# One core, a routed low-rank layer folded into one wide matmul: h transposed by transfers inside SBUF and by VectorE, three tiles behind, with the loads of x on ScalarE's queue

## The chip, the cores and the metric

The kernel runs on one core of a Trainium2 chip. Its time is the device time in microseconds (us); three runs gave 165.15, 165.2 and 165.34, so the median is 165.2 us.

## The reference

x has 128 batch rows, 32 tokens of each, 512 features. Each token goes through a linear layer with a routed low-rank part and then through a matrix of signs, and is added to x:

```
base   = x W^T
logits = x Wr^T + 5 * one_hot(itok)              # 8 experts
gates  = softmax over the top 2 logits, 0 elsewhere
h      = x A^T                                   # 8 experts x 16 ranks = 128 columns
c      = base + 2 * sum_e gates_e * (h_e B_e^T)
out    = x + (c sign) * softplus(scale)
```

All tensors are fp32.

## The kernel before

**What is folded.** Since nothing nonlinear stands between W and sign, the kernel makes M = W^T sign * softplus(scale) + I once, and B2 = B sign * 2 softplus(scale) once. A tile is one token of all 128 batch rows. For each tile it computes x times a matrix of 648 columns, which are Wr (8), A (128) and M (512): that is `wide`. It then makes the gated h (128 columns) and adds h_gated B2 to the M part: that is `lora`. Each fp32 factor is split into a high and a low part, and three products stand for one (high x high, high x low, low x high). So `wide` is 4 chunks of features x 3 products x 2 PSUM banks (392 and 256 columns) = 24 matmuls, and `lora` is 3 x 2 = 6.

**What each engine does for a tile t.** The queues run in program order and meet by semaphores.
- SyncE loads x(t) in four transfers of 64 KB (L227) and stores y (L233).
- VectorE transposes x in 32x32 blocks (L432, `turn_x`). The layout of the load makes the block transpose a full one.
- ScalarE makes the high part of x (L348, `high_x`), GpSimd the low part (L300, `low_x`).
- TensorE runs `wide` (L643) into the two banks `pair[t % 3]`. When the bank with Wr and A is done it signals `head_ready`.
- VectorE then makes logits (L516), the top two (L524, L532), the gates (L537 to L547, with ScalarE's exponential L385 between) and h_gated (L551).
- TensorE transposes h_gated against `ident` into the PSUM tile `p_ht` (L686, `turn_h`). ScalarE makes its high part ht_hi (L381), VectorE its low part ht_lo (L507, `low_h`).
- TensorE runs `lora` (L679) into the same banks, and ScalarE copies them to y (L394, L395).

**How the steps are staggered.** Step s of TensorE does the first half of wide(s), then lora(s-2), then the second half of wide(s), and last the transpose of h_gated(s-1), at the end of the step. LAG = 2 is that distance, S3 = 3 the number of buffers of everything, LEAD = 2 says that x is prepared two tiles ahead. Step s of VectorE begins with the logits of tile s-1 when TensorE starts step s. The middle steps run in a hardware loop. `finish` is a written-out end for tiles 30 and 31, in which the banks with the head come first.

**The front.** TensorE warms up on zeros (L577, into `p_b2`), makes M (L589 to L571) and B2 (L626, L630), and then `first_tile` (L668). VectorE, ScalarE and GpSimd split W, sign, B and M. softplus(scale) is a chain of eight small VectorE instructions (L448 to L457) with two exponentials on ScalarE.

## Time and profile before

| | |
|---|---|
| median of three runs | 165.2 us |
| the profiled execution, its own time | 164.64 us |
| span of that execution | 162.8 us |
| PE busy | 158.3 us (97%), 1070 matmuls |
| VectorE busy | 97.6 us (60%) |
| ScalarE busy | 66.0 us (41%) |
| GpSimd busy | 52.1 us (32%) |
| chain that ended last | PE 90% |

The page gives busy time by engine, the chain of work that ended last, groups of instructions with what ended the idle time before them, and the transfers. Matmuls are pipelined: one is shown as longer than the distance to the next. What a matmul costs is therefore read from the distance between starts, or from the pieces of the chain, and not from its duration.

### The profile page before, as it was taken

To read this page: it belongs to the slowest core of one execution; us is meant where nothing else is said; L and a number is where in the kernel's file an instruction comes from. 1 tells how busy PE (TensorE), PEld (TensorE's weight loads), DVE (VectorE), ACT (ScalarE), POOL (GpSimd) and SP (SyncE) were. 2 spreads that over 40 slices of the span, in tenths; PEclk is the share of its full clock that TensorE was granted. 3 is DMA by queue.
4 is the path that set the end of the run, shared out by engine and by line. 5 is a ranking of instruction groups with operands and counts; after the bars stand their busy time and mean duration, and the time that the engine had idled before them with its cause. 6 is when DMAs were issued, how large, how long until landed. Compare 5 with 4: busy or idle time off the path is not lost.

```text
span 162.8 us, 3711 instructions
## 1 busy us (share of the span) xinstructions
PE 158.3 (97%) x1070; PEld 153.8 (94%) x1070; DVE 97.6 (60%) x416; ACT 66.0 (41%) x177; POOL 52.1 (32%) x50
## 2 busy tenths in 40 slices
PE   7999998999999999999999999999999999999993
PEld 5788897999999999999999999999999999999992
DVE  5689997555556665554554555556665555455741
ACT  3654722434344333344444343344333344443440
POOL 2994453332222233333333322222333333333000
PEclk9999999999999999999999999999999999999998
DMA  4996323424333333334333333333333333111113
GB/s 170 380 146 136 90 82 101 131 70 146 105 122 114 124 119 115 124 129 129 129 129 127 104 101 117 112 121 123 113 123 120 128 129 129 64 64 64 68 66 129
DMA packets 29431, 19.51 MB, mean 120 GB/s; under 512 B 7248, under 2 KB 24432, under 8 KB 29424
## 3 DMA queue, kind: packets, MB, share of 16 engines
q1 hardware_dynamic: 28496, 18.23, 36.5%
q10 hardware_dynamic: 928, 1.20, 2.0%
q8 instruction: 3, 0.05, 0.1%
q14 instruction: 4, 0.03, 0.1%
HBM read 11.03 MB, written 8.39 MB: 119 GB/s over the span
## 4 chain that ended last, share of the span: by engine, by line
PE 90%; DVE 7%; issue 1%; ACT 0%; DVEq 0%
PE pair L643 66%; PE pair L679 14%; PE p_b L577 2%; PE p_ht L686 2%; PE pair L589 2%; DVE m_full L470 2%; PE pair L596 2%; PE pair L603 2%; DVE xt L432 1%; DVE wide_lo L476 1%; DVE gate L547 1%; DVE b_lo L501 0%; DVE b_lo L487 0%; DVE wide_lo L483 0%; ACT y L395 0%
## 5 line engine op out<-in xcount | busy, mean ns | idle before, releaser
L300 POOL TENSOR_TENSOR xt_lo<-xt,xt_hi 128x512 fp32r<-128x512 f32 x32 | 41.6, 1299 | 91.5 <-ACT xt_hi L348 91.5
L643 PE MATMUL pair<-wide_hi,xt_hi 128*128 128x392 f32 (+1 forms) x248 | 60.8, 321 | 0.0
L643 PE MATMUL pair<-wide_hi,xt_lo 128*128 128x392 f32 (+1 forms) x248 | 58.3, 311 | 0.0
L643 PE MATMUL pair<-wide_lo,xt_hi 128*128 128x392 f32 (+1 forms) x248 | 58.3, 311 | 0.0
L643 PEld LDWEIGHTS pair<-wide_hi,xt_lo 128*128 128x128 f32 x248 | 38.6, 188 | 0.0
L643 PEld LDWEIGHTS pair<-wide_lo,xt_hi 128*128 128x128 f32 x248 | 38.5, 188 | 0.0
L643 PEld LDWEIGHTS pair<-wide_hi,xt_hi 128*128 128x128 f32 x248 | 38.3, 189 | 0.1
L394 ACT ACTIVATE y<-pair 128x256 f32<-128x256 f32 x31 | 11.9, 384 | 44.3 <-PE pair L679 44.3
L516 DVE TENSOR_TENSOR logits<-pair,bias 128x8 f32<-128x8 f32 x32 | 5.3, 165 | 35.7 <-PE pair L643 35.7
L432 DVE STREAM_TRANSPOSE xt<-x_in 128x512 f32<-128x512 f32 x32 | 22.7, 710 | 3.7 <-DVE top L524 3.2
L348 ACT ACTIVATE xt_hi<-xt 128x512 fp32r<-128x512 f32 x32 | 20.3, 633 | 2.8 <-DVE xt L432 2.8
L381 ACT ACTIVATE ht_hi<-p_ht 128x128 fp32r<-128x128 f32 x32 | 8.9, 277 | 22.6 <-PE p_ht L686 22.6
L507 DVE TENSOR_TENSOR ht_lo<-p_ht,ht_hi 128x128 fp32r<-128x128 f32 x32 | 9.3, 290 | 13.6 <-ACT ht_hi L381 13.6
L385 ACT ACTIVATE e<-top 128x1 f32<-128x1 f32 x32 | 9.5, 296 | 14.4 <-DVE top L524 14.3
L551 DVE SCALAR_TENSOR_TENSOR h_gated<-pair,rdenom,gate 128x128 f32<-128x128 f32 x32 | 11.2, 350 | 3.3
L679 PE MATMUL pair<-b_hi,ht_hi 128*128 128x256 f32 x64 | 13.0, 281 | 0.0
L679 PE MATMUL pair<-b_lo,ht_hi 128*128 128x256 f32 x64 | 12.9, 280 | 0.0
L679 PE MATMUL pair<-b_hi,ht_lo 128*128 128x256 f32 x64 | 12.8, 279 | 0.0
L395 ACT ACTIVATE y<-pair 128x256 f32<-128x256 f32 x32 | 12.2, 380 | 1.4 <-PE pair L679 1.4
L679 PEld LDWEIGHTS pair<-b_hi,ht_hi 128*128 128x128 f32 x64 | 9.9, 188 | 0.1
L679 PEld LDWEIGHTS pair<-b_lo,ht_hi 128*128 128x128 f32 x64 | 9.9, 188 | 0.0
L679 PEld LDWEIGHTS pair<-b_hi,ht_lo 128*128 128x128 f32 x64 | 9.8, 188 | 0.0
(82 smaller groups left out, 142.0 us busy)
## 6 DMA issues: line engine op xcount, KB each, us to landing
x_in<-in_x SPq DMA_DIRECT2D x128, 64.0 KB, 1.9
out<-y SPq DMA_DIRECT2D x31, 256.0 KB, 2.1
sign_in<-in_L_ffn_sign ACTq DMA_DIRECT2D x4, 256.0 KB, 5.1
w_in<-in_L_cond_W SPq DMA_DIRECT2D x4, 256.0 KB, 4.9
a_in<-in_L_cond_A SPq DMA_DIRECT2D x4, 64.0 KB, 5.1
b_in<-in_L_cond_B SPq DMA_DIRECT2D x4, 64.0 KB, 4.2
out<-y SPq DMA_DIRECT2D x1, 128.0 KB, 1.7
out<-y ACTq DMA_DIRECT2D x1, 128.0 KB, 1.8
```

The costliest lines, as they stand in the source:

```text
L300: nc.gpsimd.tensor_tensor(xt_lo[n][:, :, :].rearrange("p j (g b) -> p g j b", g=NQ), xt[n][:, :, :, :], xt_hi[n][:, :, :].bitcast(FP32).re ...
L348: nc.scalar.activation(xt_hi[n][:, :, :].rearrange("p j (g b) -> p g j b", g=NQ), xt[n][:, :, :, :], ACT.Copy).then_inc(xt_hi_made, 1)
L381: nc.scalar.activation(ht_hi[:, :], p_ht[:, 0:P], ACT.Copy).then_inc(ht_hi_made, 1)
L385: nc.scalar.activation(e2[:, :], top[:, 0:1], ACT.Exp, bias=top[:, 1:2], scale=-1.0)\
L394: nc.scalar.activation(y[n][:, 0:Y0], pair[n][0][:, HEAD:HEAD + Y0], ACT.Copy)
L395: nc.scalar.activation(y[n][:, Y0:D], pair[n][1][:, 0:D - Y0], ACT.Copy).then_inc(y_copied, 1)
L432: nc.vector.transpose(xt[n][:, :, :, :].rearrange("p g j b -> p (g j b)"), x_in[n][:, :, :].rearrange("p g c -> p (g c)")).then_inc(xt_mad ...
L507: nc.vector.tensor_tensor(ht_lo[:, :], p_ht[:, 0:P], ht_hi[:, :].bitcast(FP32), ALU.subtract)\
L516: nc.vector.tensor_tensor(logits[:, :], pair[n][0][:, 0:E], bias[:, :], ALU.add)\
L551: nc.vector.scalar_tensor_tensor(h_gated[:, :].rearrange("p (e r) -> p e r", e=E), pair[n][0][:, E:HEAD].rearrange("p (e r) -> p e r", e=E ...
L643: last = nc.tensor.matmul(pair[n][bank][:, at0:at0 + hi - lo], l[:, k, :], w[:, k, lo:hi], start=(opens and k == 0 and l is xt_hi[n] and w ...
L679: last = nc.tensor.matmul(o, l[:, :], w[:, (0, Y0)[bank]:(Y0, D)[bank]], start=False, stop=stop, skip_group_check=True)
```

## The change

- **h goes another way.** In 29 of the 32 tiles the transpose on TensorE is gone. SyncE moves h_gated from SBUF to SBUF in four transfers (`move_h`: a block of 32 columns of all 128 partitions, 128 bytes each, goes to 32 partitions of `h_moved`), and VectorE transposes that in 32x32 blocks (`turn_h` on VectorE, into `ht` in SBUF). ht_hi and ht_lo are then made from `ht`. So lora runs three tiles behind (LAG = 3) in place of two. The last three tiles keep TensorE's transpose (`LATE = TILES - 3`), each into an own PSUM tile.
- **Four buffers** (RING = 4) replace three. PSUM holds four pairs of banks; `p_b2` and the p_ht tiles of the end are banks of these pairs, so wide(3) waits for b2_lo, and the ends of lora and of copies guard the others.
- **Loads of x**: those of tiles 0 to 3 stay on SyncE, all others are issued by ScalarE (`load`), between the exponential and the copies of y. Tile s+5 is loaded in step s.
- **Order on VectorE in a step**: logits, block transpose of h, max, ht_lo, then as before. In step 1, B2's low part and the transpose of x(3) come behind h_gated.
- **The front**: the load of scale moves from SyncE to ScalarE's queue behind the second load of sign; the softplus chain stands ahead of the last low part of W and of the transpose of x(0); B's high and low parts come ahead of those of A and Wr.
- **`finish`** holds five loras in place of four, and three transposes, in another order.

```diff
-    S3 = 3
+    RING = 4
...
-        LAG = 2
+        LAG = 3
+        LATE = TILES - 3
...
+            def move_h(q, r, d):
+                n = slot(r, d)
+                sp_eng.wait_ge(h_gated_made, RING * q + r + d + 1)
+                for i in range(NQ):
+                    sp_eng.dma_start(h_moved[n][Q * i:Q * i + Q, :, :], h_gated[n][:, Q * i:Q * i + Q])\
+                        .then_inc(h_arrived[n], 16)
             def turnover(q, r, s):
-                if s is None or s + S3 < TILES:
-                    sp_eng.wait_ge(xt_made, S3 * q + r + 1)
-                    load(q, r, S3 * q + r + S3)
+                if s is None or 0 <= s - LEAD - 1 < LATE:
+                    move_h(q, r, -LEAD - 1)
...
@@ scalar
+            def load(q, r, d):
+                n = slot(r, d)
+                act.wait_ge(xt_made, RING * q + r + d + 1 - RING)
+                for i in range(NQ):
+                    act.dma_start(x_in[n][Q * i:Q * i + Q, :, :], x_load[i, :, RING * q + r + d, :, :])\
+                        .then_inc(x_loaded[n], 16)
+            def high_h(done, late):
+                if late is None:
+                    act.wait_ge(ht_made, done - LAG + 1)
+                    nc.scalar.activation(ht_hi[:, :].rearrange("p (b g) -> p g b", g=NQ), ht[:, :, :], ACT.Copy)\
+                        .then_inc(ht_hi_made, 1)
+                else:
+                    act.wait_ge(ht_turned, late - LATE + 1)
+                    act.wait_ge(y_summed, late)
+                    nc.scalar.activation(ht_hi[:, :], p_ht[late][:, 0:P], ACT.Copy).then_inc(ht_hi_made, 1)
...
@@ vector
             for j in range(EARLY):
...
-            for j in range(EARLY, OC):
-                low_w(j)
+            low_w(1)
             dve.wait_ge(scale_loaded, 16)
             nc.vector.tensor_scalar(sp[:, 0:1], scale_in[:, :], -1.0, scale_in[:, 0:1], ALU.mult, ALU.min)\
                 .then_inc(neg_abs_made, 1)
-            turn_x(0, 0, 0, first=True)
+            low_w(2)
...
+            low_w(3)
+            turn_x(0, 0, 0, first=True)
...
+            def turn_h(q, r, s):
+                n = slot(r, -LAG)
+                dve.wait_ge(h_arrived[n], 16 * NQ * (turn(q, r, -LAG) + 1))
+                nc.vector.transpose(ht[:, :, :].rearrange("p g b -> p (g b)"),
+                                    h_moved[n][:, :, :].rearrange("p g c -> p (g c)")).then_inc(ht_made, 1)
...
@@ tensor, step
-                if has(s, -1):
-                    turn_h(done)
@@ tensor, finish
+                wide(before, range(KC - 1), (BANKS[0],), opens=True)
+                pe.wait_ge(ht_lo_made, s - 3)
+                lora((s - 4) % RING, (0, 1)).then_inc(y_summed, 1)
+                wide(before, [KC - 1], (BANKS[0],)).then_inc(head_ready, 1)
+                pe.wait_ge(xt_lo_made, s + 1)
+                pe.wait_ge(y_copied, s - RING + 1)
+                wide(r, range(KC - 1), (BANKS[0],), opens=True)
+                pe.wait_ge(ht_lo_made, s - 2)
+                lora((s - 3) % RING, (0, 1)).then_inc(y_summed, 1)
+                turn_h(s - 2)
+                wide(r, [KC - 1], (BANKS[0],)).then_inc(head_ready, 1)
+                wide(before, first, (BANKS[1],), opens=True)
+                pe.wait_ge(ht_lo_made, s - 1)
+                lora((s - 2) % RING, (0, 1)).then_inc(y_summed, 1)
+                pe.wait_ge(y_copied, s - 2)
+                turn_h(s - 1)
+                wide(before, second, (BANKS[1],))
+                wide(r, first, (BANKS[1],), opens=True)
+                pe.wait_ge(ht_lo_made, s)
+                lora(before, (0, 1)).then_inc(y_summed, 1)
+                turn_h(s)
+                wide(r, second, (BANKS[1],))
+                pe.wait_ge(ht_lo_made, s + 1)
+                lora(r, (0,)).then_inc(last_summed, 1)
+                lora(r, (1,)).then_inc(y_summed, 1)
```

ScalarE, one step inside the hardware loop, before (ht_hi is the high part of the transposed h, e the exponential, y the copies out of PSUM, xt_hi the high part of x):

```order
L381 ACTIVATE ht_hi<-p_ht 128x128 [waits ht_turned]
L384 REGISTER_ALU
L385 ACTIVATE e<-top 128x1 [waits top_made]
L394 ACTIVATE y<-pair 128x256 [waits y_stored1,y_summed]
L395 ACTIVATE y<-pair 128x256
L345 REGISTER_ALU
L348 ACTIVATE xt_hi<-xt 128x4x4x32 [waits wide_done,xt_made]
```

The same step of ScalarE now; each transfer of x is a register instruction and the issue itself:

```order
L405 ACTIVATE ht_hi<-ht 128x4x32 [waits ht_made]
L418 ACTIVATE e<-top 128x1 [waits top_made]
L391 ISA [waits xt_made]
L391 DMA x_in<-in_x 32x4x128
...
L391 DMA x_in<-in_x 32x4x128
L431 ACTIVATE y<-pair 128x256 [waits y_stored2,y_summed]
L432 ACTIVATE y<-pair 128x256
L364 REGISTER_ALU
L367 ACTIVATE xt_hi<-xt 128x4x4x32 [waits wide_done,xt_made]
```

Four issues of loads now stand between the exponential and the copies of y, and ht_hi reads SBUF in place of PSUM.

VectorE, the beginning of one step inside the loop, before (h arrives by p_ht in PSUM):

```order
L516 TENSOR_TENSOR logits<-pair,bias 128x8 [waits head_ready]
L506 REGISTER_ALU [waits logits_made]
L507 TENSOR_TENSOR ht_lo<-p_ht,ht_hi 128x128 [waits ht_hi_made]
L524 MAX top<-logits 128x8
L429 ISA [waits top_made]
L432 STREAM_TRANSPOSE xt<-x_in 128x512 [waits xt_lo_made,x_loaded1]
```

And now:

```order
L566 TENSOR_TENSOR logits<-pair,bias 128x8 [waits head_ready]
L554 ISA [waits logits_made]
L555 STREAM_TRANSPOSE ht<-h_moved 128x128 [waits h_arrived0]
L575 MAX top<-logits 128x8
L542 REGISTER_ALU
L544 TENSOR_TENSOR ht_lo<-ht,ht_hi 128x4x32 [waits ht_hi_made]
L466 ISA [waits top_made]
L468 REGISTER_ALU [waits x_loaded1]
L469 STREAM_TRANSPOSE xt<-x_in 128x512 [waits xt_lo_made]
```

One instruction is added, and it waits for the arrival of the moved h; everything behind it on VectorE waits with it. ht_lo now has two inputs in SBUF.

TensorE in `finish`, between the first lora of this part and the head of tile 31, before:

```order
L679 MATMUL pair<-b_hi,ht_lo 128x256 x2
L643 MATMUL pair<-wide_hi,xt_hi 128x392
L643 MATMUL pair<-wide_lo,xt_hi 128x392
L643 MATMUL pair<-wide_hi,xt_lo 128x392
L643 MATMUL pair<-wide_hi,xt_hi 128x392
L643 MATMUL pair<-wide_lo,xt_hi 128x392
L643 MATMUL pair<-wide_hi,xt_lo 128x392
L686 MATMUL p_ht<-ident,h_gated 128x128 [waits h_gated_made]
L643 MATMUL pair<-wide_hi,xt_hi 128x392 [waits y_copied,xt_lo_made]
```

And now:

```order
L735 MATMUL pair<-b_hi,ht_lo 128x256 x2
L699 MATMUL pair<-wide_hi,xt_hi 128x392
L699 MATMUL pair<-wide_lo,xt_hi 128x392
L699 MATMUL pair<-wide_hi,xt_lo 128x392
L699 MATMUL pair<-wide_hi,xt_hi 128x392 [waits y_copied,xt_lo_made]
```

Between a lora and the matmul that waits for the copy of that lora's bank there were six matmuls and a transpose; now there are three matmuls.

## Rows read from the trace of the kernel before

**Rows 1.** Timeline of PE, front: start us, us, engine line op, tiles, count [idle before].
```profile
25.64 0.46 PE L643 MATMUL pair<-wide_hi,xt_lo 128*128 128x392 f32 x2
26.77 0.33 PE L686 MATMUL p_ht<-ident,h_gated 128*128 128x128 f32 x1 [0.67 <-DVE h_gated L551]
...
27.23 0.46 PE L643 MATMUL pair<-wide_lo,xt_hi 128*128 128x392 f32 x2
```
**Rows 2.** Chain that ended last, steady steps: start us, us, what.
```profile
31.38 0.11 PE p_ht L686
31.49 1.79 PE pair L643 x12
33.28 0.71 PE pair L679 x6
...
35.77 0.11 PE p_ht L686
```
**Rows 3.** Timeline of all engines, one steady step.
```profile
35.60 0.27 PE L686 MATMUL p_ht<-ident,h_gated 128*128 128x128 f32 x1
...
35.68 0.17 DVE L516 TENSOR_TENSOR logits<-pair,bias 128x8 f32<-128x8 f32 x1 [1.29 <-PE pair L643]
...
36.29 0.29 DVE L507 TENSOR_TENSOR ht_lo<-p_ht,ht_hi 128x128 fp32r<-128x128 f32 x1 [0.44 <-ACT ht_hi L381]
...
36.69 0.71 DVE L432 STREAM_TRANSPOSE xt<-x_in 128x512 f32<-128x512 f32 x1
...
37.58 1.82 SPq L227 DMA_DIRECT2D x_in<-in_x  x4
...
38.40 0.38 ACT L394 ACTIVATE y<-pair 128x256 f32<-128x256 f32 x1 [1.42 <-PE pair L679]
38.42 0.35 DVE L551 SCALAR_TENSOR_TENSOR h_gated<-pair,rdenom,gate 128x128 f32<-128x128 f32 x1
...
39.66 1.29 POOL L300 TENSOR_TENSOR xt_lo<-xt,xt_hi 128x512 fp32r<-128x512 f32 x1 [3.09 <-ACT xt_hi L348]
```
**Rows 4.** Timeline of ACT and its queue, front.
```profile
8.90 0.63 ACT L335 ACTIVATE w_hi<-w_in 128x512 fp32r<-128x512 f32 x1 [0.58 <-DMA w_in<-in_L_cond_W]
9.19 0.55 ACTq L353 DMA_DIRECT2D wr_in<-in_L_cond_Wr  x1
```
**Rows 5.** Groups by line: busy us, mean ns.
```profile
L464 DVE STREAM_TRANSPOSE wrt<-wr_in 128x128 f32<-128x128 f32 x1 | 0.3, 269 | 0.0
```
**Rows 6.** Transfers by line: KB each, median us to landing.
```profile
x_in<-in_x SPq DMA_DIRECT2D x128, 64.0 KB, 1.9
...
scale_in<-in_L_ffn_scale SPq DMA_DIRECT2D x1, 0.5 KB, 5.8
```
**Rows 7.** The tile b_in: issue to landing, minimum, median, maximum.
```profile
DMA to landing us min/median/max: 3.0/4.2/4.9
```
**Rows 8.** Line 547: duration ns minimum, median, maximum, first and last start.
```profile
L547 DVE SCALAR_TENSOR_TENSOR gate<-expert_no,top_no,second x32: 225/227/1280, 25.0 to 156.9; 128x8 f32<-128x8 f32 x32
```
**Rows 9.** Timeline of POOL while line 547 took longest.
```profile
24.94 1.29 POOL L300 TENSOR_TENSOR xt_lo<-xt,xt_hi 128x512 fp32r<-128x512 f32 x1 [0.35 <-ACT xt_hi L348]
```
**Rows 10.** Timeline of DVE and PE, front.
```profile
9.56 1.18 DVE L422 TENSOR_TENSOR w_lo<-w_in,w_hi 128x512 fp32r<-128x512 f32 x1 [0.53 <-ACT w_hi L335]
...
11.48 0.15 DVE L448 TENSOR_SCALAR sp<-exp_neg 128x1 f32<-128x1 f32 x1
...
13.11 0.15 DVE L457 TENSOR_SCALAR sp<-sp 128x1 f32<-128x1 f32 x1
...
13.34 0.39 PE L569 MATMUL pair<-sign_hi,w_hi 128*128 128x512 f32 x1
```
**Rows 11.** Timeline of all engines, end: a lora, the copies of its banks.
```profile
151.13 0.40 PE L679 MATMUL pair<-b_hi,ht_lo 128*128 128x256 f32 x2
...
151.85 0.38 ACT L395 ACTIVATE y<-pair 128x256 f32<-128x256 f32 x1
```
**Rows 12.** Chain that ended last, end.
```profile
158.27 1.06 PE pair L643 x9
```

More of the change, by code:

```diff
@@ L98, in adaln_ffn_kernel @@
         ln_one = sb("ln_one", [P, 1])
-        x_in = [sb(f"x_in{n}", [P, NQ, P]) for n in range(S3)]
-        xt = [sb(f"xt{n}", [P, NQ, KC, Q]) for n in range(S3)]
-        xt_hi = [sb(f"xt_hi{n}", [P, KC, P], FP32R) for n in range(S3)]
-        xt_lo = [sb(f"xt_lo{n}", [P, KC, P], FP32R) for n in range(S3)]
+        x_in = [sb(f"x_in{n}", [P, NQ, P]) for n in range(RING)]
+        xt = [sb(f"xt{n}", [P, NQ, KC, Q]) for n in range(RING)]
+        xt_hi = [sb(f"xt_hi{n}", [P, KC, P], FP32R) for n in range(RING)]
+        xt_lo = [sb(f"xt_lo{n}", [P, KC, P], FP32R) for n in range(RING)]
         logits = sb("logits", [P, E])
@@ L164, in adaln_ffn_kernel @@
         b2_lo_made = sem("b2_lo_made")
-        x_loaded = [sem(f"x_loaded{n}") for n in range(S3)]
-        y_stored = [sem(f"y_stored{n}") for n in range(S3)]
+        x_loaded = [sem(f"x_loaded{n}") for n in range(RING)]
+        y_stored = [sem(f"y_stored{n}") for n in range(RING)]
         xt_made = sem("xt_made")
@@ L182, in adaln_ffn_kernel @@
         h_gated_made = sem("h_gated_made")
+        h_arrived = [sem(f"h_arrived{n}") for n in range(RING)]
+        ht_made = sem("ht_made")
         ht_turned = sem("ht_turned")
@@ L296, in low_x @@
             def low_x(q, r, d):
-                pool.wait_ge(xt_hi_made, S3 * q + r + d + 1)
+                pool.wait_ge(xt_hi_made, RING * q + r + d + 1)
                 n = slot(r, d)
@@ L396, in step @@
                 if has(s, LEAD):
-                    high_x(q, r, LEAD, first=(s is not None and s + LEAD < S3))
+                    high_x(q, r, LEAD, first=(s is not None and s + LEAD < RING))
             steps(act, step)
             act.wait_ge(y_copied, TILES)
-            act.dma_start(out[:, TILES - 1, Y0:D], y[(TILES - 1) % S3][:, Y0:D])\
-                .then_inc(y_stored[(TILES - 1) % S3], 16)
+            act.dma_start(out[:, TILES - 1, Y0:D], y[(TILES - 1) % RING][:, Y0:D])\
+                .then_inc(y_stored[(TILES - 1) % RING], 16)
         @block.vector
@@ L555, in step @@
                         .then_inc(h_gated_made, 1)
+                if s == 1:
+                    low_b2()
+                    turn_x(q, r, LEAD, first=True)
+                if s == TILES + 1:
+                    low_h(done, TILES - 1)
                 if s == TILES - 1 + LAG:
-                    n = (TILES - 1) % S3
+                    n = (TILES - 1) % RING
                     dve.wait_ge(last_summed, 1)
@@ L681, in lora, with turn_h @@
                 return last
-            def turn_h(done):
-                pe.wait_ge(h_gated_made, done)
-                nc.tensor.transpose(p_ht[:, 0:P], h_gated[:, :], ident[:, :]).then_inc(ht_turned, 1)
+            def turn_h(tile):
+                pe.wait_ge(h_gated_made, tile + 1)
+                nc.tensor.transpose(p_ht[tile][:, 0:P], h_gated[tile % RING][:, :], ident[:, :]).then_inc(ht_turned, 1)
             def step(q, r, s):
-                done = S3 * q + r
+                done = RING * q + r
                 if s == 0:
@@ L718, in finish @@
-                lora(slot(before, -LAG), (0, 1)).then_inc(y_summed, 1)
-                wide(before, second, (BANKS[0],)).then_inc(head_ready, 1)
-                turn_h(s - 1)
-                pe.wait_ge(xt_lo_made, s + 1)
-                pe.wait_ge(y_copied, s - S3 + 1)
-                wide(r, first, (BANKS[0],), opens=True)
-                pe.wait_ge(ht_lo_made, s - LAG + 1)
-                lora(slot(r, -LAG), (0, 1)).then_inc(y_summed, 1)
-                wide(r, second, (BANKS[0],)).then_inc(head_ready, 1)
@@ L728, in finish @@
-                turn_h(s)
-                wide(before, range(KC), (BANKS[1],), opens=True)
+                pe.wait_ge(y_copied, s - RING)
+                wide(before, range(KC - 1), (BANKS[0],), opens=True)
[4 more added lines that the diff above has]
+                pe.wait_ge(y_copied, s - RING + 1)
```

160 lines of the change are left out of this document (84 added, 76 removed).

## The prediction, made before the changed kernel was run

> **What bounds the kernel now.** I read the chain of waits first. From 27 us to the end it is one row of TensorE pieces: twelve matmuls of wide, six of lora, twelve of wide, one transpose, and again. From one transpose to the next it is 35.77 - 31.38 = 4.39 us [rows 2], and 24 wide matmuls (2 x 1.79) with a lora (0.71) make 4.29 of that. The transpose of h is the rest: 0.10 to 0.11 us on the path in every tile. Next the timeline of TensorE at the front: it has one hole, 0.67 us before the first transpose, which waits for h_gated of tile 0 [rows 1]. The timeline of a steady step then shows what the other engines do under this row, and where they have room [rows 3]. VectorE sat idle 1.29 us and GpSimd 3.09 us before their first instruction of the step, and ScalarE 1.42 us before the copies of y. So TensorE's queue is the bound, and the only question of the change is whether everything that now feeds lora and the banks stays ahead of TensorE.
>
> **What is removed.** Transposes: 32 before, 3 now. In the front, the second pair of matmuls of step 2 starts at 27.23, so its first pair stands for a start at 27.23 - 0.30 = 26.93 (a pair of 392 and 256 columns takes 1.79 / 6 = 0.30). Without the transpose of tile 0 this pair would have followed the one at 25.64 at 25.94. That is 0.99 us, the transpose's own 0.105 in it [rows 1, 2]. The other 28 give 28 x 0.105 = 2.94 us. Together 3.93 us, if nothing is late.
>
> **The steady step with the change.** I count from T, the start of a step's wide; in the step shown the transpose starts at 35.60, so T is 35.71 before. The new period is 4.28.
> - VectorE: logits at T + 0.08 (head_ready comes with the same matmul as before, now with no transpose between), 0.2 to the next instruction, the block transpose of h 0.27 [rows 5] to T + 0.55. ScalarE's ht_hi then takes 0.28 (the transpose at 35.60 shows h's path before: 36.29 + 0.29 - 35.60 = 0.98 from its start to the end of ht_lo, of which ht_hi and ht_lo with their hand-overs are 0.7). ht_lo is done at T + 1.25. Lora is due 6 x 0.30 = T + 1.79. Slack 0.5.
> - What stands behind ht_lo on VectorE moves too: the transpose of x starts at T + 1.2 (before 36.69 - 35.71 = 0.98), so h_gated, which ended 38.77 - 36.69 = 2.08 after that start, ends at T + 3.3.
> - SyncE: four issues took 1.82 us in the loop [rows 3], so the last move of h is issued near T + 4.7, and the store of y comes behind them. With the 1.9 us of the loads of x [rows 6] h has landed at T + 6.6. The moves have as many runs as these loads (128 each), of 128 bytes for 512. VectorE wants h two steps later, at 8.56 + 0.3 = T + 8.8. Slack 2.2 us, so a landing of up to 4.1 us costs nothing.
> - ScalarE gets four more issues. No loop of the trace has them there; SyncE's 1.82 us is the nearest row and the value I take. At the front an issue on ScalarE's queue began at 9.19 while an activation dispatched before it ran until 9.53, so an issue needs the queue and not the datapath [rows 4]. The exponential is dispatched when max is done, at about T + 0.7, the issues end at T + 2.55, and the copies of y, due after lora's end at 38.40 - 35.71 = T + 2.69 [rows 3], are not moved. The next wide needs that copy by T + 4.28 and it ends at 3.35. From both sides: at 0.46 each nothing; at the longest small issue of that queue, 0.55 [rows 4], the copies slip 0.2 us, still inside their slack of 0.9.
> - GpSimd's xt_lo of 1.29 us starts at 39.66 - 35.71 = T + 3.95 as before, which in the shorter period is from 0.33 before to 0.96 after the next T [rows 3].
>
> What the trace shows of the last point: the gate, normally 0.227 us, took 1.280 once, and exactly while GpSimd's xt_lo ran from 24.94 for 1.29 [rows 8, 9]. ht_lo used to read PSUM and now reads two operands of SBUF, like the gate. It is ready at T + 0.96, where xt_lo ends: at worst it slips some tenths into a slack of 0.5. The Trainium skill (SBUF — State Buffer, Who interferes with whom) says that a VectorE instruction with two SBUF inputs and a GpSimd instruction that reads SBUF exclude each other for a whole instruction; the trace agrees (1.280 beside 0.227). By that rule a start of xt_lo later by 0.5 or more would push ht_lo past the due time. I price this among the rivals.
>
> **Front.** The softplus chain of eight small instructions took 13.26 - 11.48 = about 1.8 us and ends at 13.26 before [rows 10]; it now stands ahead of the last w_lo, which ended at 10.74 and would end near 12. TensorE needs it at 13.34 [rows 10]. That cover of 1.3 us is the condition for my zero. Scale is issued about 3 us earlier, so with its 5.8 us [rows 6] it lands near 7.5, when VectorE gets to it; if not, the last w_lo slips past 13.34 one for one from a landing near 9. Bounds 0 and 1.0, I take 0. ScalarE's issues of tiles 4 to 7 delay xt_hi of tiles 2 to 4 by up to a microsecond; GpSimd's 1.29 behind it still ends before the step that needs it (tile 2: about 24.8 for 25.94). h of tile 0 is gated near 25.3, lands near 28.7, and is due at 29.5: in time. ht_lo(0) is done near 31.3, just when lora(0) is due. Cost 0.05, bounds 0 and 0.4.
>
> **End.** `finish` has two places with less cover than before.
> - The wide of tile 31 takes the banks of tile 27, whose lora is now only three matmuls ahead. In the trace a lora's last pair starts at 151.13, so the next matmul would start at 151.37; three of 0.18 later is 151.91. The copies of those banks ended at 151.85 + 0.38 = 152.23 [rows 11], plus 0.05. Stall 0.37 us.
> - The last lora needs ht_lo(31). From the start of its transpose this takes 0.98 us plus 0.05, and what stands between is the transpose (0.11) and six matmuls of 0.12 (0.71): 0.82. Stall 0.2 us. Before, nine matmuls stood there (1.06) and nothing waited [rows 12].
> Together 0.6; bounds 0.3 and 1.2. What follows the last lora is as before.
>
> **Sum.** 3.93 - 0.05 - 0.6 = 3.3 us less. The profiled execution would take 164.64 - 3.3 = 161.3 with a span of 159.5. It lies 0.56 under the median of the runs, so the median comes to 165.2 - 3.3 = 161.9 us. Its own range, with front and end at their bounds, is 161.3 to 163.2.
>
> **Rivals.**
> 1. *The moves of h land late* (slower than before). The place is VectorE's wait for h_arrived, and it feeds itself: h_gated, issues, landing, block transpose, and 3.0 us later the h_gated of two tiles on. That loop takes 1.4 + L + 3.0 + 0.1 for two periods (8.56), so it decides from a landing L of 4.1 us. The small-run transfer in the trace, B in pieces of 64 bytes, lands in 3.0 to 4.9, median 4.2 [rows 7]. At 4.9 the period grows by 0.4 us, 29 x 0.4 = 11.6: 173.5 us. At 4.2 it grows 0.05: 163.4. The gain is gone from L = 4.35. For it: shorter runs than any steady transfer. Against: B landed so in the crowded front and in 1024 runs each, not 128.
> The Trainium skill (VectorE: DVE Perf Modes, The three transpose paths) calls a plain copy with strides for the transpose 19 times slower than the transposing transfer when the innermost destination stride is large. No run here shows that; the runs here are 128 contiguous bytes on both sides, so I do not expect it.
> 2. *ScalarE becomes late* with four issues more per step: the copies of y hold the next wide, or xt_hi moves xt_lo under ht_lo. At 0.7 us an issue the slack of 0.9 is used up; at 0.75 it costs about 0.2 per tile, 5 us: 166.9. For it: the registers and issues stand in one queue with everything else. Against: 0.46 on SyncE and the overlap at the front.
> 3. *Part of the gain is eaten*, by ht_lo behind GpSimd in some steps, by the w_lo at the front or by the end: half of 2.94 plus a microsecond, 163.5 us.
> 4. *The transposes give no more than the hole*: if the 0.105 is not free once they are gone, only 0.99 - 0.6 stays: 164.8, no change.
>
> **How the numbers follow.** Forecast 0.71, rival 1 0.09 (two thirds of it slower than before), rival 2 0.05, rival 3 0.11, rival 4 0.04. A measurement of this kernel tells 0.2% (0.33 us) from no change. Faster by more: 0.71 + 0.11 + 0.03 = 0.85. No change 0.04. Slower 0.11. The range of 161.2 to 163.8 holds the forecast and rival 3 and leaves out the rest.
>
> **What would show it.** Right: the chain repeats every 4.28 us without a gap, 1041 matmuls, no wait before wide or lora in the middle; landing of the moves near 2 us; the hole at 26 gone; a wait of 0.3 to 0.4 before the first wide of tile 31 and about 0.2 before the last lora. Wrong: VectorE idle before the block transpose of h with a transfer as releaser (rival 1), TensorE waiting for the copies of y in the loop or issues on ScalarE above 0.6 (rival 2), ht_lo of over 0.5 us beside a busy GpSimd (rival 3), a period of 4.38 (rival 4).

## The result and the profile after

| | before | after |
|---|---|---|
| median of six runs, same chip | 165.09 us (164.41 to 165.34) | 166.41 us (165.75 to 167.09) |
| profiled execution, own time | 164.64 us | 166.42 us |
| its span | 162.8 us | 164.2 us |
| own time less span | 1.8 us | 2.2 us |

The ratio is 1.0096, with an interval of 1.0068 to 1.0124. I forecast 161.9 us and a gain; the change costs 1.3 us. Timed again later it gave 1.0108 (1.0071 to 1.0145). So the sign of the prediction was wrong, and the time lies 2.6 us above the upper end of its range.

The page of after, engines and chain:

```profile
PE 158.5 (97%) x1041; PEld 151.6 (92%) x1041; DVE 110.3 (67%) x445; ACT 63.6 (39%) x177; POOL 51.8 (32%) x50
...
PE 77%; SPq 7%; DVE 6%; ACT 3%; ACTq 2%; DMA 2%; issue 1%; DVEq 0%
```

1041 matmuls, as the removal of 29 transposes asks. But PE had 90% of the chain that ended last, and now has 77%; the rest is queues and VectorE. The chain of waits shows where. First the steady part: start us, us, what.

```profile
117.62 3.58 PE pair L699 x24
...
121.92 3.58 PE pair L699 x24
```

The transpose is gone and a tile takes 4.30 us, from 117.62 to 121.92. Before it took 4.38 (26 tiles from 35.71 to 149.60 of the timeline, 113.89 us). This part did what it should, for 0.084 a tile.

The same chain of after from 10 to 36 us, the front. Before, this stretch had one hole [rows 1].

```profile
12.32 3.27 DMA b_in<-in_L_cond_B
...
15.62 0.64 ACT b_hi L376
...
16.28 0.71 DVE b_lo L518
...
22.93 0.82 ACTq L391
...
25.25 0.44 ACT xt_hi L367
...
26.25 1.02 DVE second L591
...
30.43 0.90 DVE top_no L586
...
34.15 0.98 PE pair L735 x6
```

TensorE does not appear in it until the first lora at 34.15: from there back, what the others do for it sets the time. At 15 us the chain is a near tie: VectorE had waited for TensorE's last group of M until 15.38, and then only 0.15 us for b_hi at 16.28, so the late landing of B is worth 0.15 and not 3.27. In the middle stand ScalarE's issues of x (ACTq L391), which I had priced at a few hundredths. (The trace leaves numbers out of names: b_hi at L399 and b_lo at L537 are the high and low part of B2.)

**Where 1.4 us of span and 0.4 beside it went.** The starts of TensorE's milestones in the two timelines, in us:

| start of | before | after | difference of the stretch |
|---|---|---|---|
| last group of M (L569; L625) | 13.34 | 14.42 | +1.08 |
| wide of tile 1 | 22.38 | 23.74 | +0.28 |
| wide of tile 4 | 35.71 | 36.76 | -0.31 |
| wide of tile 30 | 149.60 | 149.35 | -1.30 |
| (end of) last matmul | 160.04 | 161.50 | +1.71 |
| end of span | 162.80 | 164.20 | -0.06 |

In the third stretch, the hole with its transpose (0.99), two more transposes (0.21) and one lora that moved behind it (0.72) should have given 1.92; it gave 0.31. So 1.6 was lost there, and 1.36 + 1.61 = 3.0 in the front as a whole. In the last stretch but one that same lora comes back with 0.72; the other 0.97 is waiting. Beyond the span 0.38 was added.

### The profile page after: what moved, and what is told of

The parts are those of the page before. It is cut to its first block, busy times and chain, and to the rows that moved or that the text cites. A ratio compares the mean times of both kernels' runs of the same rounds, so it can differ in the third digit from the quotient of the medians.

```text
span 164.2 us, 3633 instructions
## 1 busy us (share of the span) xinstructions
PE 158.5 (97%) x1041; PEld 151.6 (92%) x1041; DVE 110.3 (67%) x445; ACT 63.6 (39%) x177; POOL 51.8 (32%) x50
## 4 chain that ended last, share of the span: by engine, by line
PE 77%; SPq 7%; DVE 6%; ACT 3%; ACTq 2%; DMA 2%; issue 1%; DVEq 0%
PE pair L699 62%; PE pair L735 15%; SPq L255 3%; ACTq L391 2%; DMA b_in<-in_L_cond_B 2%; SPq L252 1%; DVE m_full L507 1%; SPq L233 1%; SPq L249 1%; DVE xt L469 1%; DVE second L591 1%; DVE top_no L586 1%; ACT xt_hi L367 0%; DVE b_lo L518 0%; ACT b_hi L399 0%
## 5 line engine op out<-in xcount | busy, mean ns | idle before, releaser
L699 PE MATMUL pair<-wide_hi,xt_hi 128*128 128x392 f32 (+1 forms) x248 | 58.7, 313 | 0.6 <-ACT y L432 0.3
L544 DVE TENSOR_TENSOR ht_lo<-ht,ht_hi 128x128 fp32r<-128x128 f32 x29 | 13.6, 469 | 12.9 <-ACT ht_hi L405 12.9
L405 ACT ACTIVATE ht_hi<-ht 128x128 fp32r<-128x128 f32 x29 | 12.5, 432 | 24.2 <-DVE ht L555 24.2
L735 PE MATMUL pair<-b_hi,ht_hi 128*128 128x256 f32 x64 | 13.7, 294 | 0.8 <-DVE ht_lo L544 0.8
L591 DVE TENSOR_SCALAR second<-expert_no,top_no,e 128x8 f32<-128x8 f32 x32 | 10.1, 317 | 0.0
L555 DVE STREAM_TRANSPOSE ht<-h_moved 128x128 f32<-128x128 f32 x29 | 9.0, 312 | 1.4
```

Of the source, the lines that this page charges most:

```text
L405: nc.scalar.activation(ht_hi[:, :].rearrange("p (b g) -> p g b", g=NQ), ht[:, :, :], ACT.Copy)\
L544: nc.vector.tensor_tensor(ht_lo[:, :].rearrange("p (b g) -> p g b", g=NQ), ht[:, :, :], ht_hi[:, :].bitcast(FP32).rearrange("p (b g) -> p ...
L555: nc.vector.transpose(ht[:, :, :].rearrange("p g b -> p (g b)"), h_moved[n][:, :, :].rearrange("p g c -> p (g c)")).then_inc(ht_made, 1)
L591: nc.vector.tensor_scalar(second[:, :], expert_no[:, :], top_no[:, 1:2], e2[:, 0:1], ALU.is_equal, ALU.mult).then_inc(second_made, 1)
L699: last = nc.tensor.matmul(pair[n][bank][:, at0:at0 + hi - lo], l[:, k, :], w[:, k, lo:hi], start=(opens and k == 0 and l is xt_hi[n] and w ...
L735: last = nc.tensor.matmul(o, l[:, :], w[:, (0, Y0)[bank]:(Y0, D)[bank]], start=False, stop=stop, skip_group_check=True)
```

## Why the front is late: the issue of scale

ScalarE and its queue at the start of after: start us, us, engine, line, tile.

```profile
1.66 0.46 ACTq L344 DMA_DIRECT2D scale_in<-in_L_ffn_scale  x1
...
3.27 1.28 ACT L346 ACT_TABLE_LOAD   x1 [3.27 <-issue]
4.56 1.41 ACT L349 ACTIVATE w_hi<-w_in 128x512 fp32r<-128x512 f32 x2
```

The load of scale takes 0.46 us to issue, ahead of the table load and of w_hi(0); before, the table load began at 2.62 and w_hi(0) at 4.18. VectorE and GpSimd of after then meet, and before they did not (`w_lo` is line 422 there, line 459 here):

```profile
5.15 1.28 POOL L305 TENSOR_TENSOR sign_lo<-sign_in,sign_hi 128x512 fp32r<-128x512 f32 x1
5.22 1.76 DVE L459 TENSOR_TENSOR w_lo<-w_in,w_hi 128x512 fp32r<-128x512 f32 x1 [0.47 <-ACT w_hi L349]
```

```profile
4.86 0.77 DVE L422 TENSOR_TENSOR w_lo<-w_in,w_hi 128x512 fp32r<-128x512 f32 x1
```

At 4.86 w_lo(0) slipped in ahead of GpSimd (5.06) and took 0.77. At 5.22 it started 0.07 us after GpSimd, and took 1.76. Both have two inputs in SBUF, as the gate in [rows 8, 9]. TensorE waited for it until 7.03 (before, its second group began at 6.08):

```profile
7.03 1.20 PE L652 MATMUL pair<-sign_hi,w_lo 128*128 128x512 f32 x4 [0.37 <-DVE w_lo L459]
```

From there its groups of M follow one another in 0.91 us (the first in 1.04) with no gap, until the last group at 14.42; before, they do the same from 6.08 to 13.34. So the whole 1.08 us of the first stretch is there at the second group, and the sign loads, which land later in after too, made TensorE wait for nothing.

**b_scale_act**: the kernel before, with only this load moved.

```diff
 @@ sync, before
-            sp_eng.dma_start(scale_in[:, :], scale.partition_broadcast(P)).then_inc(scale_loaded, 16)
 @@ scalar, before
+                if j == 1:
+                    act.dma_start(scale_in[:, :], scale.partition_broadcast(P)).then_inc(scale_loaded, 16)
```

> The kernel before with one part of the change alone: the load of scale goes to ScalarE's queue, behind the second load of sign. Theory A (the issue delays ScalarE's table load, so w_hi(0) comes about 0.4 us later, w_lo(0) on VectorE then starts behind GpSimd's sign_lo(0) and each waits for the other engine's whole instruction): TensorE's second group of M (the first with w_lo) starts near 7.0 instead of 6.08, and the product group at 13.34 starts near 14.4; the kernel becomes 0.7 to 1.1 us slower than before. Rival B (the late front of the changed kernel comes from the softplus chain ahead of the last w_lo, or from the order of B and A): no change, the group stays at 13.34.

Measured: 166.93 us for 165.17, ratio 1.0111 (1.007 to 1.0152). One DMA of 0.5 KB moved to another queue costs the kernel before as much as the whole change. Its rows show two ways in which it costs. The first is VectorE's w_lo(0), the second is in the chain of waits, which goes from a sign load by the last sign_hi and the exponential of the softplus chain to m_full:

```profile
5.09 1.83 DVE L423 TENSOR_TENSOR w_lo<-w_in,w_hi 128x512 fp32r<-128x512 f32 x1 [0.39 <-ACT w_hi L336]
```

```profile
2.62 8.36 DMA sign_in<-in_L_ffn_sign
...
11.00 0.55 ACT sign_hi L341
...
13.11 0.21 ACT exp_neg L357
...
15.95 0.63 DVE m_full L471
```

The sign loads issued behind scale land later too: the last sign_hi starts at 11.00 here and at 11.12 in after, at 9.44 before. Here the exponential stands behind it on ScalarE (13.11, before 11.25). The last group of M starts at 14.37, 1.03 later than before, and m_full 1.58 us after it where before it is 0.96: this is the second cost, 0.6 us. In after it is 0.96 again, since the exponential stands ahead of the last sign_hi there (10.27). How much of the 1.03 is w_lo(0) this profile can't say: w_lo(0) started 0.01 us ahead of GpSimd's instruction (5.10), took 1.83 all the same and ended at 6.92, but the first four matmuls, 0.43 to 0.60 us apart, would not have let the second group start before 6.98 either.

**a_scale_sp**: the reverse, the changed kernel with scale on SyncE behind the loads of W.

```diff
+            sp_eng.dma_start(scale_in[:, :], scale.partition_broadcast(P)).then_inc(scale_loaded, 16)
             load(0, 0, 0)
 @@ scalar
-                if j == 1:
-                    act.dma_start(scale_in[:, :], scale.partition_broadcast(P)).then_inc(scale_loaded, 16)
```

> The changed kernel with one part taken back: scale is loaded by SyncE, ahead of x(0), and no longer from ScalarE's queue. Theory A: the table load starts at 2.6 again, w_lo(0) before 4.9 to 5.0, M's last group near 13.4 in place of 14.42; 1.0 us faster than the changed kernel (about 165.4 us), unless scale lands so late that VectorE waits (then w_lo(2) moves). Rival B: M's last group stays at 14.4, time 166.4.

Measured: 165.71 us, ratio 1.0057 (1.0018 to 1.0095): 0.7 us of 1.3 back, and the two intervals overlap. Its w_lo(0) is on time again:

```profile
4.85 0.77 DVE L458 TENSOR_TENSOR w_lo<-w_in,w_hi 128x512 fp32r<-128x512 f32 x1
```

Yet its last group of M begins at 14.30, hardly better than 14.42. The chain says why, beside that of before for the same stretch:

```profile
5.08 2.04 PE pair L644 x4
```

```profile
5.08 1.17 PE pair L589 x4
```

Both start at 5.08, with data there. The first four matmuls take 2.04 us here and 1.17 there. By starts, one of 512 columns follows another after 0.43 us until 6.92, and after 0.23 later; 512 columns in 0.43 us are 1.2 in a ns, so the first stretch ran at the lower of the clock's two levels, 1.2 GHz, and the second near 2.4. The granted clock reads 1.00 in both stretches, so the profile's column does not show this. The moment at which the pace doubles differs from execution to execution, also of one kernel: see a_best below. Where scale's issue stands first this matters little, since TensorE waits for w_lo(0) until 6.96 to 7.03 anyway: in the six profiles with scale on ScalarE (after twice, b_scale_act, a_loads_sp3, a_contig, a_all_sp) the last group starts at 14.34 to 14.42. With scale on SyncE it starts at 14.30 in a_scale_sp, at 14.17 in a_both, at 14.56 in a_scale_sp_b_old (a profile of its longest execution, 167.4 us), and at 13.04 to 13.69 with the old front (below). What w_lo(0) costs is therefore the distance from where the pace alone would have the second group (5.64 to 6.92 in these profiles) to 7.0: from 0.1 to over 1 us by the execution. The mean over executions was not taken apart.

## Why the front is late: loads of x between the activations

ScalarE of after from 20 us on:

```profile
20.35 1.78 ACTq L391 DMA_DIRECT2D x_in<-in_x  x4
...
25.25 0.63 ACT L367 ACTIVATE xt_hi<-xt 128x512 fp32r<-128x512 f32 x1 [2.32 <-issue]
...
25.79 0.28 ACT L418 ACTIVATE e<-top 128x1 f32<-128x1 f32 x1
```

Its queue is putting out the loads of tile 4, four issues in 1.78 us, then makes the high part of B2 (22.24, after 1.26 us idle), and puts out the loads of tile 5, for which ScalarE is idle 2.32 us ("issue"). xt_hi(2) stood at 22.58 before and stands at 25.25 now; the exponential of tile 0 at 23.49 and now 25.79. VectorE had the top two of tile 0 ready and sat idle for that exponential:

```profile
26.10 0.15 DVE L589 TENSOR_SCALAR denom<-e 128x1 f32<-128x1 f32 x1 [1.36 <-ACT e L418]
```

Behind it h_gated(0), the low part of B2, the transposes of x(3) and the whole next step on VectorE are late; xt_lo(3) is late for step 3 (0.22), and ht_lo(0) for the first lora (0.76), both as TensorE shows it:

```profile
31.36 0.44 PE L699 MATMUL pair<-wide_hi,xt_hi 128*128 128x392 f32 x1 [0.22 <-POOL xt_lo L312]
```

```profile
34.15 0.51 PE L735 MATMUL pair<-b_hi,ht_hi 128*128 128x256 f32 x2 [0.76 <-DVE ht_lo L544]
```

**a_loads_sp3**: the changed kernel, with the loads of tiles 4 to 6 issued by SyncE, which is idle there. ScalarE begins with tile 7.

```diff
 @@ sync
+            for t in range(RING, RING + 3):
+                sp_eng.wait_ge(xt_made, t - RING + 1)
+                load(0, t, t)
 @@ scalar
             high_x(0, 1, 0, first=True)
-            load(1, 0, 0)
...
-                if has(s, 1 + RING):
+                if has(s, 1 + RING) and (s is None or s >= 2):
```

> The changed kernel with the loads of tiles 4, 5 and 6 issued by SyncE (idle there from 19 to 28 us) and ScalarE's loads beginning with tile 7 in step 2. Theory C (four issues each of tiles 4 and 5 stand ahead of xt_hi(2) and the exponential of tile 0 on ScalarE and delay everything by 2.3 us): xt_hi(2) at about 23.9 in place of 25.25, h_gated(0) ends 1.5 to 3 us earlier than 27.99, the 0.5 before the wide of tile 3 and most of the 1.0 us before the first lora go; 1.2 to 1.6 us faster, about 165.0 us. Rival D (the first lora waits for the landing of the moved h or for the longer ht_hi and ht_lo, not for ScalarE's queue): the stall before the first lora stays above 0.7 and the gain is under 0.5 us.

Measured: 165.11 us, ratio 0.9998 (0.9968 to 1.0027), 1.3 us less than after. Its chain:

```profile
23.56 8.92 PE pair L701 x60
...
32.51 0.97 PE pair L737 x6
```

60 matmuls without a gap, then the first lora at 32.51 in place of 34.15; ScalarE's xt_hi(2) is at 23.59, and VectorE does not wait for the exponential (24.12). The wait before step 3 is gone and 0.2 is left of the one before the first lora. So this cause is shown: 12 issues in the wrong queue at the wrong time, 1.3 us by the medians (the profiled execution, 164.09, was the fastest of the ten). Two instructions of VectorE stand behind GpSimd in after, `second` and `top_no`. They do so here too, and TensorE no longer waits, so they are not the cause:

```profile
24.51 1.11 DVE L593 TENSOR_SCALAR second<-expert_no,top_no,e 128x8 f32<-128x8 f32 x1
...
28.76 0.90 DVE L588 CAST top_no<-top_at 128x2 f32<-128x2 uint32 x1
```

**a_both**: a_scale_sp and a_loads_sp3 together.

> The changed kernel with both: scale loaded by SyncE ahead of x(0), and tiles 4 to 6 loaded by SyncE. Theories A and C together: 1.0 + 1.4 = 2.4 us faster than the changed kernel, 164.0 us, which is 1.0 us faster than before; what then is left against the prediction of 161.9 is the order of B (0.3), the two loop stalls (0.6), the smaller gain per tile (0.5) and the end (0.3). Rivals B and D: 166.4 to 165.9.

Measured: 164.16 us, ratio 0.9931 (0.9896 to 0.9965). The two repairs give 0.7 and 1.3 alone and 2.25 together, so within the intervals they add up. The changed kernel is now faster than before. The chain shows what is left, the other half of the front's new order:

```profile
12.62 0.15 DVE sp L493
12.78 1.13 DVE w_lo L460
```

Scale took 7.6 us from issue to landing, so the softplus chain ran until 12.78 and w_lo(3), queued behind it, started only then. TensorE's last group of M starts at 14.17, 1.09 us after the group ahead of it and not 0.91. This is the slip of the last w_lo that the prediction named and took at 0. In after itself it cost nothing: w_lo(3) ran from 12.20 to 13.66, and TensorE, late by w_lo(0), came for it at 14.42.

**a_front_old**: the whole front in the old order (scale on SyncE behind x(0), softplus behind the last w_lo and x(0), B's parts behind those of A and Wr), all else changed.

```diff
-            low_w(1)
+            for j in range(EARLY, OC):
+                low_w(j)
             dve.wait_ge(scale_loaded, 16)
...
-            low_w(2)
+            turn_x(0, 0, 0, first=True)
...
-            low_w(3)
-            turn_x(0, 0, 0, first=True)
...
             fold(0)
-            dve.wait_ge(b_hi_made, 1)
-            nc.vector.tensor_tensor(b_lo[:, :, :, :], b_in[:, :, :, :],
-                                    b_hi[:, :, :, :].bitcast(FP32), ALU.subtract).then_inc(b_lo_made, 1)
             dve.wait_ge(head_hi_made, 2)
```

> The changed kernel with its whole front put back as it was before: scale on SyncE behind x(0), the softplus chain behind the last w_lo and x(0), B behind A and Wr on ScalarE and VectorE. Theory A2 (the front's new order costs, by scale among the sign loads, by the chain ahead of the last w_lo and by B first, 1.0 to 1.5 us together): 165.0 us against 166.4 for the changed kernel, first wide of tile 1 near 22.4 to 23.2. Rival: only the scale load matters (taken back alone it gave 0.7): 165.7.

Measured: 165.06 us, ratio 1.0009 (0.9975 to 1.0042). The last group of M starts at 13.04 and the first lora at 32.33. The loads are still on ScalarE, and TensorE's waits of after are all there, 0.15 for xt_lo(3) and 0.76 for ht_lo(0): the two causes are separate. (The profiled execution, 164.1 us, was the fastest of ten.)

**a_front_old_sp3**: a_front_old with tiles 4 to 6 loaded by SyncE.

> The same with tiles 4 to 6 loaded by SyncE. If the two costs add, 163.6 us; what is left of the change is then the path of h by transfers, the loads by ScalarE from tile 7 on and the new end. Rival E (the path of h itself gives nothing, since lora waits for ht_lo or the banks): 165.2, as the kernel before.

Measured: 164.44 us, ratio 0.9963 (0.9936 to 0.999). That is 0.6 less than a_front_old, and 0.8 more than expected: here the two repairs do not give their full sum. a_both differs from it by 0.3, inside the intervals. The last parts of B landed late in this profile and TensorE waited 0.64 for b_hi at 17.01, so the old order has its own dependence on a landing. Whether that is the missing 0.8 was not tried.

**a_scale_sp_b_old**: a_scale_sp with the old order of B's parts; only the place of the softplus chain is new.

```diff
             high_x(0, 0, 0, first=True)
-            act.wait_ge(b_loaded, 16 * OC)
-            nc.scalar.activation(b_hi[:, :, :, :], b_in[:, :, :, :],
-                                 ACT.Copy).then_inc(b_hi_made, 1)
...
             nc.scalar.activation(wide_hi[:, :, 0:E], wrt[:, :, 0:E], ACT.Copy).then_inc(head_hi_made, 1)
+            act.wait_ge(b_loaded, 16 * OC)
+            nc.scalar.activation(b_hi[:, :, :, :], b_in[:, :, :, :],
+                                 ACT.Copy).then_inc(b_hi_made, 1)
```

> The changed kernel with scale loaded by SyncE ahead of x(0) and B's high and low parts behind those of A and Wr again; of the front's new order only the softplus chain ahead of the last w_lo is left. Against the kernel with scale moved back alone (ratio to before 1.0057) and the one with the whole old front (1.0009). If B's place is the rest: ratio near 1.001 (165.1 us). If the chain ahead of the last w_lo is the rest (VectorE waits there for scale and for the exponential): it stays near 1.005 (165.7 us).

Measured: 165.96 us, ratio 1.0035 (1.0001 to 1.0069), beside 1.0057 (1.0018 to 1.0095) for a_scale_sp. No difference can be told: the 0.28 us that the order of B cost in after's profile (b_in landed at 15.59, and b_hi and b_lo stood ahead of the folds) depends on a landing.

## The loop and the end

In the loop, the moves were the point of dispute. The tile h_moved in after: issues, then landing.

```profile
L264 SPq DMA_DIRECT2D h_moved<-h_gated x116: 547/597/1192, 28.0 to 150.4; - x116
...
DMA to landing us min/median/max: 1.7/1.9/3.2
```

They land in 1.9 us, as forecast, and VectorE never waits for one in the loop of after. Four issues take 2.48 us of SyncE's queue, and not the 1.82 of four loads of x, which I took; the slack held. What did take more than forecast is ht_hi (L405, median 432 ns) and ht_lo; line, tile, minimum, median and maximum:

```profile
L544 DVE TENSOR_TENSOR ht_lo<-ht,ht_hi x29: 385/398/1156, 33.7 to 153.5; 128x128 fp32r<-128x128 f32 x29
```

0.43 for 0.28 and 0.40 for 0.29: ht_lo is ready near T + 1.5 and lora is due at T + 1.8. The slack was 0.3 and not 0.5, and ht_lo's longest, 1.156, breaks it (7 of the 29 took over 0.5 us, and for 3 of these TensorE waited). That step of after:

```profile
62.19 0.38 ACT L431 ACTIVATE y<-pair 128x256 f32<-128x256 f32 x1 [2.62 <-issue]
...
63.45 1.28 POOL L312 TENSOR_TENSOR xt_lo<-xt,xt_hi 128x512 fp32r<-128x512 f32 x1 [3.63 <-ACT xt_hi L367]
...
63.83 1.16 DVE L544 TENSOR_TENSOR ht_lo<-ht,ht_hi 128x128 fp32r<-128x128 f32 x1 [0.46 <-ACT ht_hi L405]
```

Rivals 2 and 3 in one step. Three issues of x took 2.33 us once, the copies of y started at 62.19 and TensorE lost 0.3; that moved xt_hi and so GpSimd to 63.45, ahead of ht_lo at 63.83, which then had to wait (0.3 more). The Trainium skill (SBUF — State Buffer, Who interferes with whom) says that a VectorE instruction with two SBUF inputs and a GpSimd instruction that reads SBUF exclude each other; the trace agrees, 1.16 beside 0.40. All waits of the loop together are 0.87 us (0.2 at the first lora, 0.27, 0.3, and 0.08 at 73.88).

**a_contig**: the changed kernel, with ht_hi and ht_lo written without stride. It leaves out the order of the rows of h in 29 tiles.

```diff
-ht_hi[:, :].rearrange("p (b g) -> p g b", g=NQ)
+ht_hi[:, :].rearrange("p (g b) -> p g b", g=NQ)
 (and ht_lo the same)
```

> The changed kernel with ht_hi and ht_lo of the moved tiles written in the order in which they are read (runs of 32, no stride of 4 elements); the rows of the moved tiles' low-rank part come out in another order. Theory F (the stride of 16 bytes is why ht_hi takes 0.43 us where the copy from PSUM took 0.28, and ht_lo 0.39 for 0.29): 0.28 and 0.29 again, ht_lo ready 0.25 us earlier in each step, the two waits for ht_lo inside the loop (0.3 and 0.1 us) gone, the wait before the first lora 0.2 us shorter; 0.3 to 0.6 us faster than the changed kernel. Rival: reading SBUF instead of PSUM is what costs, and both times stay.

Measured: 166.08 us, ratio 1.0063 (1.003 to 1.0096), beside 1.0108 (1.0071 to 1.0145) for after on the same chip at the same time (**after_again**: 166.59 us). ht_hi has a median of 312 ns here for 432, and ht_lo:

```profile
L544 DVE TENSOR_TENSOR ht_lo<-ht,ht_hi x29: 291/293/900, 33.7 to 153.8; 128x128 fp32r<-128x128 f32 x29
```

So the stride costs 0.12 on ScalarE and 0.10 on VectorE. In the time that is worth about 0.5 us, not told from nothing by these intervals; the first lora still waits (34.06), since the front feeds it late. The waits inside the loop that were to go are still there, three of about 0.2: ht_lo is ready to start earlier and meets GpSimd's xt_lo all the same (0.88 to 0.90 us long at 37.70, 63.72 and 132.73). The stride is a smaller cause than the front.

> The changed kernel as it is, beside the others on one chip: ratio to before near 1.0096 (interval 1.0068 to 1.0124 the first time). TensorE's first matmuls of M start between 4.8 and 5.3 us, and its spacing of 512-column matmuls falls from 0.43 to 0.23 us at a moment that differs by up to 1.5 us between executions.

Its profile has the same front: last group of M at 14.35, first lora at 34.57 after a wait of 0.75.

**a_all_sp**: all loads of x on SyncE, behind one another with the moves; ScalarE issues none.

```diff
 @@ sync, turnover
+                if has(s, 2):
+                    if s is None or s + 2 >= RING:
+                        sp_eng.wait_ge(xt_made, RING * q + r + 2 + 1 - RING)
+                        load(q, (r + 2) % RING, RING * q + r + 2)
 @@ scalar
-            load(1, 0, 0)
...
-                if has(s, 1 + RING):
-                    load(q, r, 1 + RING)
```

> The changed kernel with all loads of x issued by SyncE, none by ScalarE. An issue of a move of h took SyncE 0.62 us in the changed kernel and a load 0.46: with the store of 0.6, a step needs 4 x 0.62 + 4 x 0.46 + 0.6 = 4.9 us of SyncE's queue where TensorE needs 4.30. Theory: the period becomes 4.9 us and the time grows by some 25 x 0.6 = 15 us, near 180. Rival: issues overlap with other waits of the queue and it stays near 166.

Measured: 193.58 us, ratio 1.172 (1.1626 to 1.1814). SyncE's queue in it:

```profile
84.96 1.84 SPq L233 DMA_DIRECT2D x_in<-in_x  x4
86.84 2.51 SPq L264 DMA_DIRECT2D h_moved<-h_gated  x4
89.60 0.39 SPq L239 DMA_DIRECT2D out<-y  x1
```

and the group of the block transpose of h:

```profile
L556 DVE STREAM_TRANSPOSE ht<-h_moved 128x128 f32<-128x128 f32 x29 | 9.0, 312 | 30.6 <-DMA h_moved<-h_gated 30.2
```

From one store (84.16) to the next it is 5.4 us, of which 4.7 are issues: more than the 4.30 that TensorE needs. I had expected 4.9 a step and 180 us; the 0.7 us between the issues, a step, was not in my sum. VectorE waits 30.2 us for the moves, and with that rival 1 exists, with a queue for its cause and not a landing. So in the loop the loads do belong on ScalarE's queue, and only in the front do they harm.

**The end.** The chain of after:

```profile
151.12 0.77 PE pair L735 x6
...
152.30 0.28 ACT y L432
...
152.72 1.85 PE pair L699 x9
```

The wait for the copy of tile 27's banks is there, as forecast: the matmul at 152.07 is followed at 152.72 and not 152.25, 0.47 us (I had 0.37). The waits for ht_lo(29) and, before the last lora, for ht_lo(31) are about 0.15 and 0.25 (I had 0 and 0.2). After each wait the first matmuls start a little further apart, together some 0.1 us; that makes 0.97.

**a_best**: a_front_old_sp3, with three matmuls more between that lora and the reuse of its banks.

```diff
                 wide(before, [KC - 1], (BANKS[0],)).then_inc(head_ready, 1)
+                wide(before, range(1), (BANKS[1],), opens=True)
...
-                wide(before, first, (BANKS[1],), opens=True)
+                wide(before, range(1, 2), (BANKS[1],))
```

> The same, and in the end one chunk of the other bank of tile 30 (three matmuls of 0.12) moved ahead of the wide of tile 31, to cover the copies of tile 27's banks. Theory: the wait for these copies was 0.47 us in the changed kernel, and 0.36 of it goes; what h of tile 31 loses in cover has 0.7 us of slack. 163.3 us. Rival: the end is set by the transposes of the last three tiles, and it only moves the wait: no difference to the kernel without it.

> The version with the old front, tiles 4 to 6 loaded by SyncE and the covered copies at the end, again with more rounds: 0.3 to 0.6% faster than the kernel before (its first ratio was 0.9956, interval 0.9922 to 0.9991).

Measured: 164.09 us, ratio 0.9956 (0.9922 to 0.9991), and again, as **a_best_again**, 164.07 us, 0.9943 (0.991 to 0.9976): about 1 us faster than before and 2.4 faster than after, and the only repeated win. It is not told apart from a_both (0.9931) or a_front_old_sp3 (0.9963): the repair of the end is worth some tenths at most, and the 163.3 us expected for it was missed by 0.8. The chain of a_best_again shows the end without the wait for y, and with one for ht_lo(29) in its place, 0.27 us (the lora behind it takes 0.98 where 0.71 is usual):

```profile
148.93 2.68 PE pair L698 x15
...
153.20 0.30 DVE ht_lo L547
153.54 0.98 PE pair L734 x6
```

The two profiles of this one kernel also show the pace at the start. The first is the chain of a_best, the second TensorE's timeline in a_best_again:

```profile
5.07 1.52 PE pair L644 x4
```

```profile
5.84 1.08 PE L651 MATMUL pair<-sign_hi,w_lo 128*128 128x512 f32 x4
```

In a_best matmuls of 512 columns start 0.43 apart until 6.2 us, and its second group (L651) begins at 6.43; in the other the pace doubled at 5.15 and that group begins at 5.84. The same code, 0.6 us apart. At the first lora nothing is left of it (31.84 and 31.80), because in a_best_again TensorE waits for wide_lo meanwhile, and the spans are 161.4 and 161.3.

## Why the prediction was wrong

My sum for the profiled execution was 161.3, and it was 166.42. The 5.1 us, term by term:

- **Front: I said 0.05, it cost 3.0, which is 2.9 more.** This step failed, and alone it turns the sign. I priced scale by its landing only, "issued about 3 us earlier, so it lands near 7.5", and never the 0.46 us that the issue adds ahead of the table load, w_hi(0) and two sign loads: by w_lo(0), which then met GpSimd, 1.08 at the last group of M, and 1.8 us when done alone. Scale landed near 8.1, I took 7.5. I did write that the issues of tiles 4 to 7 delay xt_hi of tiles 2 to 4 "by up to a microsecond"; xt_hi(2) slipped by 2.7, half of it the loss that the front already had (1.36) and half two groups of four issues ahead of it, and the exponential went with it. What I left out is the exponential: I followed the delay by xt_hi to GpSimd alone, while VectorE sat idle 1.36 us for e(0) and gated h of tile 0 by 27.99 and not by 25.3, 2.7 us late. Its next step had no idle time to catch up in. That was 1.5 us (0.49 at step 3 and 1.0 at the first lora), which a_loads_sp3 gave back but for 0.2. The order of B was priced at nothing and cost 0.3 in that execution. The bounds of 0 and 0.4 had no row behind them. My own range was also summed wrongly: with the fronts at 1.0 and 0.4 and the end at 1.2 the gain is 3.93 - 2.6 = 1.33, so its upper end is 163.9 and not 163.2; the result lies far outside both.
- **Gain per tile: I said 0.105, it was 0.084.** The transpose's piece of the chain is 0.105 to 0.11 [rows 2], but the distance from tile to tile was 4.38 before (113.89 / 26) and not the 4.39 of two rows, and is 4.30 now, not 4.28. Over the 26 tiles of the loop that is 0.55 us.
- **Loop: I said no wait, there were 0.87 us.** ht_hi and ht_lo were taken at the durations of unstrided forms. My slack of 0.5 was 0.3. Rival 2 came once; the sign of rival 3, ht_lo over 0.5 us beside a busy GpSimd, came in 7 of 29 tiles and made TensorE wait in three.
- **End: I said 0.6, it cost 0.97.** The mechanism and both places were right; a third, 0.15 before the lora of tile 29, was missing.
- **Around the span: I said as before, it is 0.38 more.** 1.8 us in every run of before, 2.2 in every run of every kernel of the changed form. b_scale_act has 1.8 and a_front_old 2.2, so it comes neither with scale nor with the order of the front. What causes it was not tried and stays open.

These are 2.92 + 0.55 + 0.87 + 0.37 + 0.38 = 5.09 us. Against the medians the miss is only 4.5, since the profiled execution of before lay 0.45 under the median of its six runs, and that of after lay on it.

What was right: 1041 matmuls; the steady period, with no gap in all but four places; landing of 1.9 us; the hole at 26 us gone; the wait before tile 31; rival 1 not coming while SyncE has no loads. Rival 4 falls, the period did shrink. By its own loop rival 1 was also priced a little low: a landing of 4.2 us makes the period (4.5 + 4.2) / 2 = 4.35, which is 0.07 a tile and 163.9 us, not 163.4. Rival 3 named ht_lo behind GpSimd, a w_lo in the front and the end; but the w_lo was the last and not the first, and its 1.6 us are a third of what was missing. What I gave 0.71 was a steady state that I had worked out beside a front that I had not.

a_scale_sp gave back 0.7 and b_scale_act lost 1.8 by the same move. The rows say why they need not agree: in b_scale_act the late sign load costs 0.6 by the softplus chain, in after it costs nothing; and a_scale_sp's profile lost at the lower pace (second group at 6.92) what w_lo(0) gave back. Not settled: how the pace is spread over executions, and whether the pace at the start depends at all on what a kernel does.

## What to carry to other kernels

An issue of a DMA costs the queue that issues it about half a microsecond, and it must be counted as an instruction of that engine: in the loop it vanished in a slack, in the front it stood ahead of the activations that everything waits for. Before the profit of a steady state is booked, redo the start-up step by step on every queue, because a change that gives 0.08 us a tile, 2.2 us in 26 tiles, was lost by one load and a dozen issues that stood in front of the wrong activations there. A transfer of 16 KB between partitions, 128 bytes a run, is a working replacement for a transpose on a bound TensorE, if the queue that issues it has 2.5 us a tile to spare.

## What the runs showed of the hardware that I had not expected

- Four moves of 16 KB from SBUF to SBUF hold SyncE's queue for 2.48 us (one issue 0.547 to 1.192, median 0.597), four loads of 64 KB for 1.82 to 1.84.
- TensorE's matmuls of 512 columns started 0.43 us apart until some time between 4.9 and 6.9 us from the start, and 0.23 apart from then on, with a granted clock of 1.00 in the records of both; for one kernel it was 6.2 and 5.15. It moves the last group of M by 0.6 us there, and the span by 0.1.
- A start 0.07 us after GpSimd's made VectorE's instruction 1.76 us long. 0.20 us ahead of GpSimd's it took 0.77, but 0.01 ahead of it (b_scale_act) 1.83.
- Writing 128 x 128 with a stride of four elements costs ScalarE 0.12 us and VectorE 0.10.
